# A selective scan's inputs: the convolution as diagonal matmuls, and GpSimd's work on ScalarE and VectorE

## The reference

```python
xz = x @ in_proj_w.T                       # of which the kernel's third phase computes x_in, 512 channels
xc = conv_general_dilated(transpose(x_in), conv_w, (1,), [(3, 0)], feature_group_count=512) + conv_b
x_in = silu(transpose(xc))                 # u
x_dbl = x_in @ x_proj_w.T                  # 33 columns: dt_raw, Bp, Cp
dt = clip(softplus(dt_raw @ dt_proj_w.T + dt_proj_b), 1e-4, 10.0)
# the scan reads dt, dt * u, Bp, Cp
```

## Time and profile before

| | us |
|---|---|
| median of 3 runs (lowest, highest) | 6645.64 (6645.48, 6649.22) |
| the profiled execution, its own time | 6640.38 |
| its span, first to last instruction | 6638.7 |
| the phase of the change, about 3711 to 4399 of the span | 688 |
| one turn of its loop, 3923.99 to 4005.35 | 81.4 |
| in that turn busy: DVE, ACT, POOL, PE | 73.2, 51.4, 38.8, 34.5 |

### The profile page before, as it was taken

The page is one execution under the profiler, slowest core; times in us unless marked ns, Lnnn a source line. Parts: engine busy times, 40 slices in busy tenths (PEclk is TensorE's granted clock), DMA queues, the critical chain, the costliest instruction groups (busy, mean ns, idle before and its releaser), DMA issues. The chain is left out here.

```text
span 6638.7 us, 95330 instructions
## 1 busy us (share of the span) xinstructions
PE 5016.2 (76%) x27420; PEld 2058.7 (31%) x27420; DVE 4896.9 (74%) x9319; ACT 3869.7 (58%) x6353; POOL 1429.3 (22%) x1658
## 2 busy tenths in 40 slices
PE   6979799797979799795999644426666666667778
PEld 3333333333333333333666322201111111114555
DVE  6666564756666564755888688979999999996768
ACT  5555555555555555553444466667777777774443
POOL 0000000000000000000111244444433434434421
PEclk8989899898989999897999866655555555558999
DMA  0000000000000000001111233331111111114432
GB/s 23 1 13 1 14 1 1 14 1 14 1 14 1 14 1 1 7 1 36 41 41 43 64 116 115 113 97 43 42 44 44 42 43 42 44 40 151 154 98 70
DMA packets 198908, 273.62 MB, mean 41 GB/s; under 512 B 13989, under 2 KB 157989, under 8 KB 192454
## 3 DMA queue, kind: packets, MB, share of 16 engines
q1 hardware_dynamic: 181190, 252.90, 12.6%
q10 hardware_dynamic: 17408, 16.78, 0.7%
HBM read 151.14 MB, written 118.49 MB: 41 GB/s over the span
## 5 line engine op out<-in xcount | busy, mean ns | idle before, releaser
L643 DVE TENSOR_REDUCE at_nmax<-at_ps_s 128x1 f32<-128x1024 f32 x1024 | 1248.9, 1224 | 640.7 <-PE at_ps_s L342 639.4
L485 ACT ACTIVATE at_probsT<-at_ps_t 128x512 f32<-128x512 f32 x2048 | 1111.5, 594 | 831.5 <-PE at_ps_t L367 831.4
L1928 PE MATMUL sc_da<-sc_parts,sc_sel 24*128 24x512 bf16 x1024 | 527.0, 616 | 596.8 <-DVE sc_decayed L2017 507.1
L2027 DVE CUSTOM_DVE_ANT_0 sc_state<-sc_xd,sc_decayed 128x256 f32<-128x256 f32 x2048 | 787.6, 426 | 137.8 <-POOL sc_xd L1902 137.8
L1902 POOL TENSOR_SCALAR sc_xd<-sc_xd 128x1024 f32<-128x1024 f32 x512 | 584.4, 1141 | 942.5 <-ACT sc_xd L1987 942.5
L1981 ACT ACTIVATE sc_da<-sc_da,sc_a_col 128x1024 f32<-128x1024 f32 x512 | 557.1, 1088 | 375.4 <-PE sc_da L1928 375.3
L2017 DVE SCALAR_TENSOR_TENSOR sc_decayed<-sc_da,sc_state 128x256 f32<-128x256 f32 x2048 | 766.3, 416 | 6.4 <-ACT sc_da L1981 6.4
L363 PE MATMUL at_ps_t<-at_qkT 108*128 108x512 bf16 x2048 | 663.9, 385 | 64.9 <-ACT at_probsT L485 35.5
L342 PE MATMUL at_ps_s<-at_qkT 108*128 108x512 bf16 x2048 | 666.5, 410 | 26.3 <-DVE at_nmax L643 12.1
L1987 ACT ACTIVATE sc_xd<-sc_ps_du,sc_bt 128x512 f32<-128x512 f32 x1024 | 644.4, 684 | 0.0
L376 PE MATMUL at_ps_o<-at_probsT,at_v 128*32 128x256 f32 x8192 | 628.3, 390 | 1.4 <-ACT at_probsT L485 1.4
(11 more groups left out here) (307 smaller groups left out, 8059.1 us busy)
## 6 DMA issues: line engine op xcount, KB each, us to landing
dt_parts<-si_pt SPq DMA_DIRECT2D x64, 384.0 KB, 2.6
du_parts<-si_pu SPq DMA_DIRECT2D x64, 384.0 KB, 3.2
sc_parts<-dt_parts SPq DMA_DIRECT2D x128, 192.0 KB
sc_parts<-du_parts SPq DMA_DIRECT2D x128, 192.0 KB
u_tok<-si_ut SPq DMA_DIRECT2D x8, 2048.0 KB, 8.3
y<-sc_yo SPq DMA_DIRECT2D x256, 64.0 KB
so_yin<-y SPq DMA_DIRECT2D x32, 512.0 KB
so_uin<-u_tok SPq DMA_DIRECT2D x32, 512.0 KB
```

The source lines that it names most:

```text
L485: nc.scalar.activation(probsT[:, c % RING, u * HALF:(u + 1) * HALF], ps_t[u][:], ACT.Exp).then_inc(s_exp, 1)
L643: nc.vector.tensor_reduce(nmax[:, par, t:t + 1], ps_s[t % 2][:], AX_X, ALU.max, negate=True).then_inc(s_max, 1)
L1928: dt_done = nc.tensor.matmul(da[q % 2][:, j], sel[0:KR, :], parts[0:KR, h, q % HP * 2 + j], start=True, stop=True)
L2027: nc.vector._custom_dve(bass.dve_ops.TENSOR_ADD_SAT, out=state[:, j % SRING, ch], in0=xd[:, q % RING, j % 2, ch], in1=decayed[:, ch], s0=S ...
```

## The change

- The convolution moves from DVE to PE. DVE builds 16 diagonal matrices of 128x128 once (`taps`, the identity times one tap of one block of channels). Per item, block m and half of the tokens, four f32 matmuls, one a tap, add up in one of the banks `ps[0]` to `ps[3]`. PE does `convolved(b, m - 1)` after the projection of block m. From the fifth half on it waits for the silu that empties the bank.
- The silu reads the bank, in eight halves instead of four whole blocks, and adds the convolution's bias.
- One plus the exponential moves from POOL to ACT, in turn with the logarithms.
- The two subtractions of first parts move from POOL to DVE (`rests`). DVE's order of a turn becomes products(t), rests(t - 1), third_parts(t - 2), and `dt` and `du` get four buffers instead of two. `pt` and `pu` keep two.
- POOL keeps one memset.

```diff
@@ -1383,9 +1384,8 @@
-        one_col = sb("one_col", [P, 1])
+        taps = sb("taps", [P, KI, CONV, P])
         xc = sb("xc", [P, KI, PAD + T])
-        acc = sb("acc", [P, KI, T])
...
-        dt = sb("dt", [P, 2, DI])
-        du = sb("du", [P, 2, DI])
+        dt = sb("dt", [P, RING, DI])
+        du = sb("du", [P, RING, DI])
...
         def _(pool):
             nc.gpsimd.memset(xc[:, :, 0:PAD], 0.0).then_inc(s_zero, 1)
-            nc.gpsimd.memset(one_col[:], 1.0)
-            pool.drain()
-
-            with pool.Fori(0, B) as b:
-                for t in range(TB):
-                    pool.wait_ge(s_ex, b * TB + t + 1)
-                    nc.gpsimd.tensor_tensor(ex1[:, t], ex[:, t], one_col[:].broadcast_to([P, DI]),
-                                            ALU.add).then_inc(s_ex1, 1)
-                for t in range(TB):
-                    w, i = t % 2, b * TB + t
-                    pool.wait_ge(s_t1, i + 1)
-                    nc.gpsimd.tensor_tensor(dt[:, w], dt[:, w], pt[:, w, 0], ALU.subtract).then_inc(s_tr, 1)
-                    pool.wait_ge(s_u1, i + 1)
-                    nc.gpsimd.tensor_tensor(du[:, w], du[:, w], pu[:, w, 0], ALU.subtract).then_inc(s_ur, 1)
...
+            def convolved(b, m):
+                pe.wait_ge(s_xc, b * 8 + 2 * m + 2)
+                for hf in range(NHALF):
+                    n = m * NHALF + hf
+                    if n >= 4:
+                        pe.wait_ge(s_u, b * 8 + n - 3)
+                    for j in range(CONV):
+                        last = nc.tensor.matmul(ps[n % 4][:], taps[:, m, j, :],
+                                                xc[:, m, j + hf * HALF:j + (hf + 1) * HALF],
+                                                start=(j == 0), stop=(j == CONV - 1))
+                    last.then_inc(s_conv, 1)
...
                         last.then_inc(s_in, 1)
+                    if m >= 1:
+                        convolved(b, m - 1)
+                convolved(b, KI - 1)
                 for hf in range(NHALF):
                     for m in range(KI):
-                        if hf == 0:
-                            pe.wait_ge(s_u, b * KI + m + 1)
+                        if hf == 0 and m in (0, KI - 1):
+                            pe.wait_ge(s_u, b * 8 + (6 if m == 0 else 8))
...
             def gated(b):
-                for m in range(KI):
-                    act.wait_ge(s_conv, KI * b + m + 1)
-                    nc.scalar.activation(u[:, m], acc[:, m], ACT.Silu).then_inc(s_u, 1)
+                for n in range(2 * KI):
+                    m, hf = n // NHALF, n % NHALF
+                    act.wait_ge(s_conv, 2 * KI * b + n + 1)
+                    nc.scalar.activation(u[:, m, hf * HALF:(hf + 1) * HALF], ps[n % 4][:], ACT.Silu,
+                                         bias=cb[:, m:m + 1]).then_inc(s_u, 1)
...
                 for t in range(TB):
+                    nc.scalar.activation(ex1[:, t], ex[:, t], ACT.Copy, bias=1.0).then_inc(s_ex1, 1)
                     nc.scalar.activation(lg[:, t], ex[:, t], ACT.Ln, bias=1.0).then_inc(s_lg, 1)
...
-            def conv(b):
-                for m in range(KI):
-                    dve.wait_ge(s_xc, 2 * KI * b + 2 * m + 2)
-                    nc.vector.tensor_scalar(acc[:, m], xc[:, m, 0:T], cw[:, m, 0:1], cb[:, m:m + 1], ALU.mult, ALU.add)
-                    dve.drain()
-                    for j in range(1, CONV):
-                        last = nc.vector.scalar_tensor_tensor(acc[:, m], xc[:, m, j:j + T], cw[:, m, j:j + 1],
-                                                              acc[:, m], ALU.mult, ALU.add)
...
+            for m in range(KI):
+                for j in range(CONV):
+                    last = nc.vector.tensor_scalar(taps[:, m, j, :], identf[:], cw[:, m, j:j + 1], None, ALU.mult)
+            last.then_inc(s_taps, 1)
...
+            def rests(b, t):
+                w, r, i = t % 2, t % RING, b * TB + t
+                dve.wait_ge(s_t1, i + 1)
+                nc.vector.tensor_tensor(dt[:, r], dt[:, r], pt[:, w, 0], ALU.subtract).then_inc(s_tr, 1)
+                dve.wait_ge(s_u1, i + 1)
+                nc.vector.tensor_tensor(du[:, r], du[:, r], pu[:, w, 0], ALU.subtract).then_inc(s_ur, 1)
...
-                for t in range(1, TB):
-                    products(b, t)
-                    third_parts(b, t - 1)
-                third_parts(b, TB - 1)
-
-            conv(0)
+                for t in range(1, TB + 2):
+                    if t < TB:
+                        products(b, t)
+                    if t <= TB:
+                        rests(b, t - 1)
+                    if t >= 2:
+                        third_parts(b, t - 2)
+
             with dve.Fori(1, B) as b:
                 dt_taken(b - 1)
                 arguments()
-                conv(b)
                 tokens(b - 1)
```

More of the change, by code:

```diff
@@ L1367, in ssm_input_phase @@
     identf, _ = ident
+    RING = 4
     B, T, D, TB, KD, DI, KI, S, CONV = sh.B, sh.T, sh.D, sh.TB, sh.KD, sh.DI, sh.KI, sh.S, sh.CONV
@@ L1407, in ssm_input_phase @@
         s_zero = sem("pads_cleared")
+        s_taps = sem("taps_ready")
         s_x = sem("x_loaded")
@@ L1422, in ssm_input_phase @@
         s_arg = sem("softplus_arg_ready")
-        s_ex = sem("softplus_exp_ready")
         s_lg = sem("softplus_log_ready")
@@ L1522, in _ @@
             pe.wait_ge(s_wr, 3)
+            pe.wait_ge(s_zero, 1)
+            pe.wait_ge(s_taps, 1)
+            def convolved(b, m):
[9 more added lines that the diff above has]
+                    last.then_inc(s_conv, 1)
             with pe.Fori(0, B) as b:
@@ L1610, in exps @@
                 act.drain()
-                nc.scalar.activation(ex[:, t], ex[:, t], ACT.Exp, scale=-1.0).then_inc(s_ex, 1)
+                nc.scalar.activation(ex[:, t], ex[:, t], ACT.Exp, scale=-1.0)
             def logs(b):
@@ L1623, in split @@
                 act.wait_ge(s_std[w], b * TB * 8 + t // 2 * 16)
-                nc.scalar.copy(pt[:, w, 0], dt[:, w]).then_inc(s_t1, 1)
-                nc.scalar.copy(pu[:, w, 0], du[:, w]).then_inc(s_u1, 1)
+                nc.scalar.copy(pt[:, w, 0], dt[:, r]).then_inc(s_t1, 1)
+                nc.scalar.copy(pu[:, w, 0], du[:, r]).then_inc(s_u1, 1)
                 act.wait_ge(s_tr, i + 1)
-                nc.scalar.copy(pt[:, w, 1], dt[:, w]).then_inc(s_t2, 1)
+                nc.scalar.copy(pt[:, w, 1], dt[:, r]).then_inc(s_t2, 1)
                 act.wait_ge(s_ur, i + 1)
-                nc.scalar.copy(pu[:, w, 1], du[:, w]).then_inc(s_u2, 1)
+                nc.scalar.copy(pu[:, w, 1], du[:, r]).then_inc(s_u2, 1)
             x_stored(0)
@@ L1663, in _ @@
             dve.wait_ge(s_w, 7 * 16)
-            dve.wait_ge(s_zero, 1)
-            def conv(b):
-                for m in range(KI):
-                    dve.wait_ge(s_xc, 2 * KI * b + 2 * m + 2)
-                    nc.vector.tensor_scalar(acc[:, m], xc[:, m, 0:T], cw[:, m, 0:1], cb[:, m:m + 1], ALU.mult, ALU.add)
-                    dve.drain()
-                    for j in range(1, CONV):
-                        last = nc.vector.scalar_tensor_tensor(acc[:, m], xc[:, m, j:j + T], cw[:, m, j:j + 1],
-                                                              acc[:, m], ALU.mult, ALU.add)
-                        if j < CONV - 1:
-                            dve.drain()
-                    last.then_inc(s_conv, 1)
+            for m in range(KI):
+                for j in range(CONV):
+                    last = nc.vector.tensor_scalar(taps[:, m, j, :], identf[:], cw[:, m, j:j + 1], None, ALU.mult)
+            last.then_inc(s_taps, 1)
             def dt_taken(b):
@@ L1700, in products @@
             def products(b, t):
-                w, i = t % 2, b * TB + t
+                w, i = t % RING, b * TB + t
                 dve.wait_ge(s_raised, i + 1)
@@ L1714, in products @@
                 nc.vector.tensor_tensor(du[:, w], dt[:, w], ut[:, t], ALU.mult).then_inc(s_du, 1)
+            def rests(b, t):
+                w, r, i = t % 2, t % RING, b * TB + t
+                dve.wait_ge(s_t1, i + 1)
+                nc.vector.tensor_tensor(dt[:, r], dt[:, r], pt[:, w, 0], ALU.subtract).then_inc(s_tr, 1)
+                dve.wait_ge(s_u1, i + 1)
+                nc.vector.tensor_tensor(du[:, r], du[:, r], pu[:, w, 0], ALU.subtract).then_inc(s_ur, 1)
             def third_parts(b, t):
-                w, i = t % 2, b * TB + t
+                w, r, i = t % 2, t % RING, b * TB + t
+                dve.wait_ge(s_tr, i + 1)
+                dve.wait_ge(s_ur, i + 1)
                 dve.wait_ge(s_t2, i + 1)
-                nc.vector.tensor_tensor(pt[:, w, 2], dt[:, w], pt[:, w, 1], ALU.subtract).then_inc(s_t3, 1)
+                nc.vector.tensor_tensor(pt[:, w, 2], dt[:, r], pt[:, w, 1], ALU.subtract).then_inc(s_t3, 1)
                 dve.wait_ge(s_u2, i + 1)
-                nc.vector.tensor_tensor(pu[:, w, 2], du[:, w], pu[:, w, 1], ALU.subtract).then_inc(s_u3, 1)
```

(1 more changed line is left out.)

## The result

| | before | after |
|---|---|---|
| median, us (of 4 runs each) | 6645.56 | 6890.26 (6881.11 to 6894.31) |
| ratio, with its 95% interval | | 1.0367 (1.0349 to 1.0385) |
| own time of the profiled execution | 6640.38 | 6881.11 |
| turn of the loop, mean of seven | 81.9 | 112.1 |

A forecast was written before the change was run, and what follows sets the result against it. One chain through PE, DVE and ACT sets the turn, with DVE's queue the bound at the first split. Item 0 +22.4, seven turns +204.7 and last tokens +5.9 make 233, so 6878 us, 3.5% slower; range 6785 to 6930.

The forecast's parts named there:

- first split: ACT's first split in a turn, behind all silus: predicted to move from 37.75 to 64.6 us, 26.9 later.
- tail: Eight token blocks from first split to next dt_raw: 46.0 us predicted against 43.6, with six store-bound steps of 6.3.
- item 0: First item, before the turns: convolution now follows PE's projection instead of running beside it on DVE; +22.4 us.
- item 7's tokens: Token work after the last dt_raw copy: 68.3 us predicted against 62.4, +5.9.
- diagonals are cheap: Rival on PE: a convolution matmul takes one instruction instead of two, 112 us less in all, 6766; chance 0.04.
- The second half of the convolution: PE idles 15 us until ACT's first silu, behind all logarithms; then 14.0 plus 1.8 cold start, ending at 63.8.
- The stores: In the tail, splits wait for stores to free `pt`, landing 3.2 us after issue: 6.3 a step against DVE's 5.15.
- Before, DVE's slow products hid the stores: Tail term: the prediction's reason why the kernel before did not show the new wait for stores.
- The stores don't bind: Rival on the tail: buffers come free in time, tail 35.2 instead of 46.0, 86 us less, 6792; chance 0.1.
- The rival in which the second half ran at the lower level to its end: PE clock rival: only the convolution's second half at half speed, 98 us more, 6976; chance 0.08 shared with 7100 case.
- Freed port: Rival on DVE: without POOL's contention, PE's work hidden and stores never awaited, a turn takes 73.7 us, 6586; chance 0.03.

The follow-up runs named there:

- the one-tap kernel: The changed kernel with the matmul of one tap instead of four, three quarters of the convolution's products left out: 6728.75 us, 1.0118.
- the kernel with half of the silus first: The changed kernel with ACT's first four silus ahead of the logarithms and the other four behind them: 6815.17 us, 1.025.
- the silus between the splits: Kernel with convolution on VectorE, POOL idle and four part buffers, plus one silu behind each of the first four splits: 6569.61 us, 0.9882.

## Why the prediction was right, by its steps

| step, us from dt_raw | predicted | shown turn |
|---|---|---|
| projection begins | 4.70 | 4.71 |
| last projected bank | 32.7 | 32.45 |
| exponentials end | 36.1 | 35.5 |
| logarithms end | 46.0 | 45.4 |
| convolution's second half ends | 63.8 | 63.56 |
| first split | 64.6 | 64.19 |
| tail, split to dt_raw | 46.0 | 47.19 |
| turn | 110.6 | 111.38, mean 112.1 |
| item 0, more than before | 22.4 | 22.0 |
| item 7's tokens | 68.3 | 68.7 |

*PE.* The convolution's matmuls cost what the projection's do, 3.5 us a bank pair; "diagonals are cheap" falls, and the one-tap kernel shows that every one of them is on the chain.

*ACT.* I priced one plus the exponential at the pitch of a logarithm, 0.534, between bounds of 0.534 and 0.64. All sixteen follow at 0.52, and they need one table load, not one each.

*Item 0.* PE begins 1.6 us earlier in the span of after than in that of before; dt_raw is 20.5 later, 22.0 without that. The sixteen diagonals, priced at nothing, take 3.2 us of DVE, and PE's turning of the inputs waits 1.1 us for them, where it waited 0.7 for a DMA.

*The second half of the convolution.* It waits as forecast (15.13, released by the silu); its cold start costs 2.0 in the turn shown and 1.5 to 2.4 over the seven, 1.8 in the mean, which is what I had. The measure is item 0, where the same instructions follow a stop of 2.77 at full speed:

```profile
3756.25 13.98 PE L1519 MATMUL si_ps<-si_xc,si_taps 128*128 128x512 f32 x32 [2.77 <-ACT si_u L1598]
```

Shown by the kernel with half of the silus first: the place in ACT's queue makes the wait.

*The stores.* The wait is where I put it, the size was off: a step was to be 6.3 and is 6.48, since from DVE's last third part to the copy that reopens the buffer 3.43 us pass (3972.59 less 3966.76 less 2.4), not 3.25. That is 1.1 a tail, 9 in all. "Before, DVE's slow products hid the stores" leaves out the old order, as the kernel before with four buffers says above. "The stores don't bind" (6792) falls; the kernel with four buffers, which makes it true, gave 6801. The fit in the Trainium skill, DMA: Bandwidth & Descriptors, section on the anatomy of one DMA, is made for DMAs that GpSimd issues, which the prediction didn't say; for this size it gives an estimate of 2.9 us. The stores here are issued by SyncE and landed in 3.2, the median of the earlier trace rows and of the kernel after. By the fit a step would be 6.0, and the runs with two buffers say 6.48.

*The clock.* The rival in which the second half ran at the lower level to its end (6976) falls: the row of 15.99 says 2 us more than at full speed, not 12.2. I had a cold projection in the bounds and not in the sum. In four of the seven turns it came (8.82 to 9.01 for the first sixteen instructions instead of 7.13), and these turns are 112.6 to 113.0 long: 5 us in all. That item 0 would start its second half warm after 2.77 us came true here; with the convolution alone on TensorE it did not (17.04, see the last section), so that term held by luck.

*The sum.* Item 0 +20.5 in the span, seven turns +211.6 (784.9 against 573.3), the last tokens +6.3: 238.3 of the 240.7 by which the profiled executions differ; predicted were 233. The turns make up the miss: 0.8 each in the shown one (5.5), the cold starts (5), less 3.7, since I took 81.36 for a turn of before whose mean is 81.9. Against the medians 4 us more are missing: the profiled execution of after is 9.2 below its median, and I had added 5.2.

*Freed port.* As a forecast it was wrong, since the first split stood at 64.2 and not before 35.4. As a mechanism it is real. The Trainium skill, GPSIMD Engine Reference, section Specifications, has GpSimd and VectorE share SBUF interfaces and contend where VectorE's instruction has two SBUF inputs; the trace agrees (1.64 us beside POOL, 0.69 without), and the kernel with VectorE's convolution and four buffers is 53 us faster than before, with POOL's work gone (onto ACT and DVE, in the new order) and the buffers as its only edits: four buffers by themselves gave nothing. It reached 6592 where my rival had 6586 with PE's convolution hidden, which no kernel here showed.

What stays open: speed and order in the stores' wait, as said above. The 3.43 us between issue and copy were seen as a whole; how much of it is the semaphore's way was not measured apart. And the earlier phases differ between kernels by up to 18 us in the span (PE's transposes of the weights, the phase's first, stand at 3720.24, 3724.76 and 3737.97 in three kernels whose earlier phases are the same code), so medians of kernels less than that apart are read here by their turns.

## What to carry to other kernels

Work moved from an engine with a queue of its own to one that another engine's queue empties brings that queue's order with it: list, for each bank or buffer, what stands in the releasing queue ahead of the release. A slow instruction, or a longer row of instructions between two uses of a buffer, can hide a store; before either is changed, compare the distance between store and reuse with the landing time, and give the buffers first. Here the good half of the change (GpSimd out of VectorE's way) was worth 53 us with four buffers for the parts instead of two, and cost 28 us without them; the best kernels, with the silus between the splits too, take 6569 to 6570 us, 1.2% less than before.

## What the runs showed of the hardware

The granted clock in four stretches of the shown turn of the changed kernel, the first of them in PE's stop, and in one of the kernel with half of the silus first (columns as in group 2):

```profile
3936.00:3938.90 2.90, 0.00 (x0) 0.00 (x0) 0.55 (x1) 2.87 (x5) 0.00 (x0) 0.50 0.00 0
3939.00:3942.00 3.00, 3.00 (x4) 1.44 (x5) 0.00 (x0) 1.55 (x3) 0.00 (x0) 0.50 0.00 0
3942.00:3945.00 3.00, 3.00 (x7) 1.18 (x6) 0.00 (x0) 0.31 (x1) 0.00 (x0) 0.83 0.00 0
3945.00:3954.80 9.80, 9.80 (x24) 4.08 (x22) 0.00 (x0) 1.75 (x3) 0.00 (x0) 1.00 0.00 0
```

```profile
3926.40:3929.40 3.00, 3.00 (x4) 1.45 (x5) 0.00 (x0) 2.90 (x5) 0.00 (x0) 0.50 0.00 0
```

At the end of the stop the clock is at 0.50, 1.2 GHz; the first 3 us of matmuls all run at that level, and within the next 3 us it rises to 2.4 GHz. I had not expected that a stop of 5.20 us costs as much as one of 15.13: 15.38 to 16.26 us for the 32 instructions in seven turns, against 15.48 to 16.42, with the same mean of 15.77. A stop cut by two thirds gives back its length, and nothing of the cold start. The length of a stop doesn't even tell whether there is one. After the 2.77 us of item 0 the changed kernel runs at full speed, 13.98; the kernel with the convolution alone on TensorE, whose projection had itself started cold, doesn't:

```profile
3761.32 17.04 PE L1535 MATMUL si_ps<-si_xc,si_taps 128*128 128x512 f32 x32 [2.77 <-ACT si_u L1614]
```

Over the first 3 us of these instructions the granted clock is 0.50 in this kernel and 1.00 in the changed one. What makes the difference was not tested.
